# A GRU's recurrent products with 64 moving columns in place of 8

## What is computed

```
def step(h, xt):                       # h: (8, 256), 512 steps one after the other
    xr_t, xz_t, xn_t = xt              # input projections of this step
    r = sigmoid(xr_t + h @ w_hr.T + b_hr)
    z = sigmoid(xz_t + h @ w_hz.T + b_hz)
    n = tanh(xn_t + r * (h @ w_hn.T + b_hn))
    h_new = (1.0 - z) * n + z * h
```

## Time and profile before

| | us |
|---|---|
| median of 3 runs | 1646.11 |
| lowest and highest | 1638.33, 1646.47 |
| span of the profiled execution, first to last instruction | 1636.9 |
| PE busy | 1365.0 (83%) |
| DVE busy | 1143.2 (70%) |
| ACT busy | 704.4 (43%) |
| POOL busy | 434.8 (27%) |

### The profile page before, as it was taken

The page is one execution under the profiler, slowest core; times in us unless marked ns, Lnnn a source line. Parts: engine busy times, 40 slices in busy tenths (PEclk is TensorE's granted clock), DMA queues, the critical chain, the costliest instruction groups (busy, mean ns, idle before and its releaser), DMA issues. The chain is left out here.

```text
span 1636.9 us, 65673 instructions
## 1 busy us (share of the span) xinstructions
PE 1365.0 (83%) x27355; PEld 1027.9 (63%) x27370; DVE 1143.2 (70%) x5594; ACT 704.4 (43%) x2475; POOL 434.8 (27%) x818
## 2 busy tenths in 40 slices
PE   5888888878878888888888887379999999999886
PEld 4667777767767777777777776245556555555443
DVE  5767777777777777777777776557576776776485
ACT  3333223222222222222222222136777777777765
POOL 2001111111111111111111111364245535522354
PEclk6555555555555555555555555578999999999998
DMA  5200000000000000000000000068537735742001
GB/s 120 29 4 5 5 7 5 5 6 5 5 5 7 5 5 6 5 5 7 5 5 7 5 5 7 7 140 139 73 66 110 98 58 89 106 68 29 1 14 39
DMA packets 68941, 53.70 MB, mean 33 GB/s; under 512 B 12686, under 2 KB 68390, under 8 KB 68646
## 3 DMA queue, kind: packets, MB, share of 16 engines
q1 hardware_dynamic: 66470, 49.32, 18.3%
q10 hardware_dynamic: 2176, 0.20, 0.1%
HBM read 31.84 MB, written 15.47 MB: 29 GB/s over the span
## 5 line engine op out<-in xcount | busy, mean ns | idle before, releaser
L731 PE MATMUL PS<-GB,W 128*128 128x8 f16 x18432 | 575.7, 168 | 177.3 <-DVE GB L1041 173.2
L731 PEld LDWEIGHTS PS<-GB,W 128*128 128x128 f16 x18432 | 532.6, 104 | 285.9 <-DVE GB L1041 281.1
L935 ACT ACTIVATE tr<-PS 128x16 f32<-128x16 f32 x512 | 94.7, 185 | 490.2 <-PE PS L731 490.2
L2383 DVE TENSOR_REDUCE MX<-PS 128x1 f32<-128x512 f32 (+3 forms) x352 | 220.0, 635 | 114.8 <-PE PS L1842 111.6
L2121 ACT ACTIVATE PT<-PS 128x512 f32<-128x512 f32 (+1 forms) x352 | 193.2, 566 | 114.7 <-PE PS L1858 110.1
L937 ACT ACTIVATE tz<-PS 128x16 f32<-128x16 f32 x512 | 94.2, 184 | 192.0 <-PE PS L731 192.0
L1027 DVE SCALAR_TENSOR_TENSOR u_<-tr,PS 128x16 f32<-128x16 f32 x512 | 87.4, 171 | 126.0 <-PE PS L731 114.0
L685 POOL TENSOR_TENSOR rt<-mv,eps 128x1 f32<-128x1 f32 x96 | 18.4, 191 | 553.1 <-DVE mv L1052 553.1
L1034 DVE SCALAR_TENSOR_TENSOR zg<-tz,HR 128x16 f32<-128x16 f32 x512 | 90.1, 176 | 81.5 <-ACT tz L937 81.4
L1839 PE MATMUL PS<-KS,QS 99*128 99x256 bf16 (+3 forms) x512 | 134.0, 314 | 12.8 <-DVE MX L2383 8.5
L1855 PE MATMUL PS<-QS,KS 102*128 102x256 bf16 (+3 forms) x512 | 128.8, 302 | 6.2 <-ACT PT L2121 5.6
(11 more groups left out here) (393 smaller groups left out, 2496.8 us busy)
## 6 DMA issues: line engine op xcount, KB each, us to landing
QS<-q_parts SPq DMA_DIRECT2D x90, 128.0 KB, 11.0
KS<-k_parts SPq DMA_DIRECT2D x90, 128.0 KB, 13.1
q_parts<-PQ SPq DMA_DIRECT2D x16, 384.0 KB, 10.4
k_parts<-PK SPq DMA_DIRECT2D x16, 384.0 KB, 3.3
X<-XM SPq DMA_DIRECT2D x32, 64.0 KB
out_dram<-X SPq DMA_DIRECT2D x8, 256.0 KB, 2.3
XM<-in_L_attn_x_dram SPq DMA_DIRECT2D x16, 80.0 KB
s_hh<-in_L_attn_w_hh_dram SPq DMA_DIRECT2D x1, 768.0 KB, 5.4
```

Of the source, the lines that this page charges most:

```text
L731: return pe.matmul(bank[:, p, at:at + B], W[:, kc, w:w + P], state[:, part, kc, :], start=False, stop=True, skip_group_check=True)
L935: act.activation(as_states(tr), now(pR), ACT.Tanh, scale=gate_scale).then_inc(hn_tr.sem, 1)
L2383: dve.tensor_reduce(MX[:, g % 2, heads[0]:heads[-1] + 1, NT - 1 - it], p_x[:, k % 2, 0:len(heads) * w].rearrange("p (a w) -> p a w", w=w), ...
```

## The change

`product` moves 64 columns (WIDE) that end with the 8 of the state in place of these 8: the 56 columns before them in the ring are read too. They are older states or other parts of the ring. The result goes to 64 columns of PSUM that end with the step's own 8. The other 56 results are added into columns that lie before: those of earlier steps of the bank, whose values were taken already, and a lead of 64 columns that is never read. For that each chunk's block in a bank grows from U * B = 32 columns to BLOCK = 96, with the 32 used ones at its end; `inject` still writes 32 columns, and the readers on ACT and DVE take their 16 from the new places.

GB gets a lead of 64 columns and is made in the earlier scope (GBF with the lead, GB as a view). POOL sets all 1600 columns of it to zero in the set-up, behind `identh`, and DVE waits for this before it clears the first state. Number, order and semaphores of the products stay as they are, and so does everything beside the steps.

```diff
+RG = 3
+LAG = 2
+WIDE = 64
+LEAD = 64
+BLOCK = LEAD + U * B
...
+        GBF = sb(gru_scope, "GB", [P, LEAD + RG * 2 * HC * GS * B], FP16)
+        GB = GBF[:, LEAD:].rearrange("p (r h c s b) -> p r h c s b", r=RG, h=2, c=HC, s=GS)
...
+                pool.memset(GBF[:, :], 0.0).then_inc(consts.sem, 1)
...
-            GB = sb(ctx, "GB", [P, RG, 2, HC, GS, B], FP16)
...
-                def product(gate, p, k, state, mc, kc, W, part):
+                def product(gate, p, k, ring, slot, mc, kc, W, part, wide=WIDE):
                     bank, g = gates[gate]
                     w = (HC * g + mc) * P
-                    at = (mc * U + k) * B
-                    return pe.matmul(bank[:, p, at:at + B], W[:, kc, w:w + P], state[:, part, kc, :],
+                    end = LEAD + mc * BLOCK + (k + 1) * B
+                    state = LEAD + (((ring * 2 + part) * HC + kc) * GS + slot + 1) * B
+                    return pe.matmul(bank[:, p, end - wide:end], W[:, kc, w:w + P], GBF[:, state - wide:state],
                                      start=False, stop=True, skip_group_check=True)
...
-                            o = bank[:, p, first + mc * U * B:first + (mc + 1) * U * B]
+                            at = first + LEAD + mc * BLOCK
+                            o = bank[:, p, at:at + U * B]
...
-                XN_AT = U * NSTEP
+                XN_AT = HC * BLOCK
...
-                    now = lambda bank: bank[:, p, 0:U * NSTEP].rearrange("p (c u b) -> p c u b", c=HC, u=U)[:, :, k, :]
+                    now = lambda bank: bank[:, p, 0:HC * BLOCK].rearrange("p (c u b) -> p c u b", c=HC, b=B)[:, :, LEAD // B + k, :]
...
+                dve.wait_ge(consts.sem, 15)
                 dve.memset(GB[:, RG - 1, 0, :, GS - 1, :], 0.0).then_inc(g1_ready.sem, 1)
...
-                    hn, xn = [pN[:, p, i * U * NSTEP:(i + 1) * U * NSTEP].rearrange("p (c u b) -> p c u b", c=HC, u=U)[:, :, k, :]
+                    hn, xn = [pN[:, p, i * HC * BLOCK:(i + 1) * HC * BLOCK].rearrange("p (c u b) -> p c u b", c=HC, b=B)[:, :, LEAD // B + k, :]
                               for i in range(2)]
```

More of the change, by code:

```diff
@@ L449, in build @@
         SLOTS = GS
-        RG = 3
-        LAG = 2
         ctx = ExitStack()
@@ L573, in build @@
             xl = Signal(loads_ih.sem, 1, 16)
-            fsc = Signal(consts.sem, 1, 14)
+            fsc = Signal(consts.sem, 1, 15)
             fps = Signal(bias_ps.sem, 1, 1)
@@ L757, in steps @@
                     n = first + (s + 1) if isinstance(first, int) else pe.snap(first + (s + 1))
-                    state = GB[:, ring, :, :, s - 1, :] if s else GB[:, (ring - 1) % RG, :, :, GS - 1, :]
+                    state = (ring, s - 1) if s else ((ring - 1) % RG, GS - 1)
                     pe.wait_ge(g1_ready.sem, n)
                     for w in by_g1:
-                        product("r", p, k, state, *w, 0)
+                        product("r", p, k, *state, *w, 0)
                     for w in by_g1[:3]:
-                        product("n", p, k, state, *w, 0)
+                        product("n", p, k, *state, *w, 0)
                     pe.wait_ge(g2_ready.sem, n)
                     for w in by_g2:
-                        last = product("r", p, k, state, *w, 1)
+                        last = product("r", p, k, *state, *w, 1)
                     last.then_inc(r_ps.sem, 1)
                     for w in by_g1[3:]:
-                        product("n", p, k, state, *w, 0)
+                        product("n", p, k, *state, *w, 0)
                     for w in by_g2:
-                        last = product("n", p, k, state, *w, 1)
+                        last = product("n", p, k, *state, *w, 1)
                     last.then_inc(hn_tr.sem, 1)
                     for w in by_g1:
-                        product("z", p, k, state, *w, 0)
+                        product("z", p, k, *state, *w, 0)
                     for w in by_g2:
-                        last = product("z", p, k, state, *w, 1)
+                        last = product("z", p, k, *state, *w, 1)
                     last.then_inc(z_ps.sem, 1)
```

## The result

The changed kernel takes 1685.55 us (median of 4 runs, 1680.39 to 1688.12) against 1644.86 before (4 runs, 1638.33 to 1646.47): a ratio of 1.025, 95% interval 1.0228 to 1.0272. The forecast was 1690 us, slower. In the profiled runs the span goes from 1636.9 to 1684.3 us, +47.4.

A forecast was written before the change was run, and what follows sets the result against it. Bound by 512 recurrence steps, each a chain of PE products at half clock and small DVE and ACT instructions. Span 1636.9 + 38 (steps) + 6 (ramp) = 1681 us, with +9.2 to run time 1690 us; range 1642 to 1800.

The forecast's parts named there:

- The clock rises and stays: Recurrence loop: PE's clock goes from 0.50 to full within the first dozen steps and holds to the loop's end.
- The ramp: Loop start: about 6 steps still at half clock, each +0.96 us, costing +6 us.
- Rival 2: Loop: clock rises late or falls between, 100 to 300 steps at 2.90 us, 1770 to 1960 us; chance 0.09.
- Start to start: Loop products: 64 columns at full clock start every 29 ns, against 27.2 before.
- The end: Loop products: one 64-column product lasts 192 ns at full clock, against 168 before, +24 ns.
- u later by 65 ns: Each step: u, which waits for n's products, starts 65 ns later after the first product.
- tz by 87: Each step: tz, which waits for z's products, starts 87 ns later after the first product.
- n held by tz: ACT in each step: if n cannot start sooner than 0.09 us behind tz, the step grows by 87 ns, not 65.
- The 75 ns: Growth of each step, taken as the middle of 65 and 87 ns; over 512 steps +38 us.
- The 9.2 us: Whole kernel: added to the forecast span to get the time, as the median run lay +9.2 above the profiled span.
- POOL's memset is hidden: Set-up: the added 1600-column memset takes 1.5 us, hidden in 10.67 us; without that cover it would cost 1.5.
- Rival 3: Loop products: 64 columns start every 26.7 ns or less, so not slower, 1640 to 1654 us or 1632; chance 0.12.

The follow-up runs named there:

- e1: Changed kernel with 8 moving columns in place of 64, new layout, memset and wait kept; ratio 0.9998 to the kernel before.
- e2: Changed kernel with z's 12 products at 8 columns, r and n at 64; ratio 1.0717 to the kernel before.
- e5: Changed kernel with z's 12 products at 48 columns, r and n at 64; ratio 1.0235 to the kernel before.
- e9: e7's widths without its added products; 1748.12 us, ratio 1.0619 to the kernel before.
- e6: Changed kernel with 56 columns in all products; ratio 1.003 to the kernel before.
- e3: Changed kernel with 48 columns in all products; ratio 1.0005 to the kernel before.
- e4: Changed kernel with 32 columns in all products; ratio 1.0012 to the kernel before.
- e7: Changed kernel, r and n behind the low part at 8 columns, other products 48, unread 320-column products added in each step's tail; 1626.69 us, ratio 0.9899 to before.
- e8: Changed kernel with 96 columns and a lead of 96; one run, 1931.84 us.

## Why the prediction was right, step by step

- **The clock rises and stays**: right. It was the step that no row of before showed; e1 shows that the width causes it. The ramp was set at 6 us and is about 0.9, which the first step shows (2.65 us from its first product to its state, 1.77 before): the clock rose behind the first step, after a stretch with the injections ahead of the loop in it (PE busy 3.38 of 3.41 us), which the prediction had not counted. The reason given for its staying was that PE pauses only about half a microsecond a step. It does, but this is not what tells a clock that holds from one that falls. In the rows below PE waits for GB 219.5 us in 445 steps of the changed kernel, 0.49 a step; 210.5 us in 420 steps of e2, 0.50, and there the clock falls again and again; 237.2 us in some 448 steps of e5, 0.53, and there it holds to within 30 us of the loop's end. e2 and e5 differ in z's columns alone. That the clock held was forecast rightly, on a reason that would have had e2's hold as well. Rival 2's clock that falls between is what e2 and e9 show with fewer columns.

```profile
L737 PE MATMUL PS<-GB,W 128*128 128x64 f16 x16020 | 544.4, 193 | 219.5 <-DVE GB L1049 219.5
```
```profile
L737 PE MATMUL PS<-GB,W 128*128 128x64 f16 x10080 | 421.1, 204 | 210.5 <-DVE GB L1049 210.1
```
```profile
L737 PE MATMUL PS<-GB,W 128*128 128x64 f16 x10740 | 390.9, 193 | 237.2 <-DVE GB L1049 237.2
```

(The three are the changed kernel, e2 and e5, from 100 to 1000 us; a step has 36, 24 and 24 products of 64 columns.)

- **Start to start**: 29 ns forecast from the four 128-column products of the earlier trace rows, 29 measured in the median (29.3 in the mean of the step shown, whose first gap is longer). The end: 192 forecast, 193 measured.
- **u later by 65 ns**: 0.07. **tz by 87**: 0.10, a little more.
- **n held by tz**: it is, in every step, but ACT starts n 0.080 behind tz and not 0.09, and an n that starts so close lasts 207 ns in place of 216. The two make the hold cheap, 0.010 us (e5). The 75 ns taken from 65 and 87 became 81, 41.5 us for 38: 0.069 by u, 0.020 by the hold, less 0.009 by the shorter n. The 75 was the middle of two cases, taken for want of a row; that it came so near is in part luck, as it stands for none of these three terms.
- **The sum**: 1636.9 + 41.5 + 0.9 is 1679.3 us of span; the profiled 1684.3 has 5 more behind the loop, which come and go in kernels of either kind. The forecast's change was 38 + 6 = 44 us, the medians differ by 40.7: the ramp was 5 us too long and the steps 3.5 too short. The 9.2 us that the forecast added for the way from span to time is not such a way: in the experiments every run's time lies 1.7 to 1.8 us above its own span, and the changed kernel's profiled run took 1686.01 us with its span of 1684.3. The rest is the spread of the runs, of which the profiled one of before was among the fastest. That the total still came near is in part luck: the 5 us behind the loop fell to the changed kernel.
- **Two readings** in the prediction are off and carry nothing: the row of the clock has 25 slices at 0.5, not 24, and 0.107 us is 128 columns at 1.2 GHz, not a figure of the earlier trace rows.
- **POOL's memset is hidden**: it took 1.42 us (row below), and POOL's next work (L157, L152 before) started at 15.01 us as before.

```profile
4.30 1.42 POOL L304 MEMSET GB<- 128x1600 f16 x1
```

- **Rival 3** was wrong for 64 columns and right, as no change, below. It had the break-even at 26.2 ns; 56 columns start every 26 and cost nothing a step (e6). The Trainium skill's rule of one figure for 1 to 64 columns ("TensorE: Matmul & The Clock Gate", section "Back-to-back issue gap") agrees with e2, e3 and e4 for 8, 32 and 48 columns, 25 ns each, and not with 64: 29 ns, the columns and 2 to 3 beside. Nor would 25 ns have given rival 3's -0.027 us a step: with 48 columns the low part of the state holds r, and the step falls by 0.011.

Not shown is what in the products' activity the clock follows: the runs give widths at which it held and at which it fell, no more.

## What to carry to other kernels

Price a full clock by the chain and not by the busy share: where a loop waits for short products one after another, each already starting as fast as weights load, doubling the clock moved the start to start from 27 to 25 ns and took 12 ns off a product of 32 columns (188 to 176), 0.036 us a step (e4), while the 64 columns that bought a steady clock here start every 29 ns and last 193. Give the columns to products off the chain: work in the tail of the step, and operands as wide as their start-to-start floor hides, held the clock in e7 without a place in the chain, for 1% of the time. And look at the second branch: a column cost 0.010 us a step from 56 to 64, where n's 24 products carry nearly all of it, and 0.015 from 64 to 96, where z's 36 do.

## What was not expected of the hardware

- At full clock products of 8, 32 and 48 columns start every 25 ns alike, with 166, 176 and 183 ns each; 56 columns 26, 64 columns 29, 96 columns 42.7.
- Twelve of 36 products narrowed from 64 to 8 columns (e2) turned a clock that held for 1037 us into one that changed between 1.00 and 0.50 through the loop; 48 columns for the same twelve (e5) held it for 997 us.
- ACT starts a 16-column activation 0.080 us behind another when both are ready (after, e8), and the second, n, lasts 207 ns where it takes 216 with more room.
